# A graph layer with a mixture of experts: eleven dense sets of four tiles in place of thirteen

## The reference, cut to what matters

```python
h = layernorm(x) @ W
x = x + segment_sum(h[dst] * edge_weight[:, None], src) + bias
xn = layernorm(layernorm(x)) * gamma + beta
logits = xn @ Wr + br                       # 8 experts
w = softmax(top_2(logits))                  # spread over 8 columns, zero elsewhere
for e in range(8):
    y += (gelu(xn @ W1[e] + b1[e]) @ W2[e] + b2[e]) * w[:, e, None]   # 256 -> 512 -> 256
x = x + y
```

## Time and profile before

| | |
|---|---|
| median of 3 runs | 3774.95 us (3774.81 to 3778.23) |
| the profiled execution | 3771.83 us, of which 3770.1 us span |
| mean granted TensorE clock | 0.933 |
| busy in the span | TensorE 86%, VectorE 66%, GpSimd 64%, ScalarE 36% |

### The profile page before, as it was taken

The page is one execution under the profiler, slowest core; times in us unless marked ns, Lnnn a source line. Parts: engine busy times, 40 slices in busy tenths (PEclk is TensorE's granted clock), DMA queues, the critical chain, the costliest instruction groups (busy, mean ns, idle before and its releaser), DMA issues. The chain is left out here.

```text
span 3770.1 us, 77968 instructions
## 1 busy us (share of the span) xinstructions
PE 3237.5 (86%) x21468; PEld 2119.4 (56%) x21468; DVE 2486.9 (66%) x6355; ACT 1339.0 (36%) x2814; POOL 2402.3 (64%) x2251
## 2 busy tenths in 40 slices
PE   6679777644799999999999999999999999999997
PEld 3445444422455555555555555555555555567886
DVE  9699655534666676667666676666676667655664
ACT  1353766630122222223222222222222222255664
POOL 1151388877766766666667667676667676674555
PEclk8899888876899999999999999999999999999999
DMA  4342010103333333333334333333333333454554
GB/s 151 98 131 71 27 26 25 26 14 89 110 104 105 107 103 107 104 107 100 110 94 117 95 111 105 102 104 107 101 105 109 102 108 103 122 157 99 90 88 67
DMA packets 258290, 358.36 MB, mean 95 GB/s; under 512 B 86661, under 2 KB 199370, under 8 KB 257994
## 3 DMA queue, kind: packets, MB, share of 16 engines
q0 software_dynamic: 108032, 247.79, 25.2%
q1 hardware_dynamic: 106968, 64.44, 6.4%
q10 hardware_dynamic: 42996, 42.43, 3.5%
HBM read 290.79 MB, written 63.57 MB: 94 GB/s over the span
## 5 line engine op out<-in xcount | busy, mean ns | idle before, releaser
L804 POOL DMA_INDIRECT area<-h_table,listed x1664 | 1672.3, 1005 | 748.8 <-issue 482.4
L1901 PE MATMUL twin<-area 128*128 x2800 | 1024.1, 410 | 174.5 <-issue 148.8
L1903 PE MATMUL twin<-area 128*128 x2800 | 811.1, 290 | 0.0
L977 ACT ACTIVATE area<-twin,b_t 128x512 f32<-128x512 f32 x208 | 142.9, 687 | 1340.9 <-PE twin L1954 793.8
L1901 PEld LDWEIGHTS twin<-area 128*128 x2800 | 289.9, 104 | 575.6 <-issue 336.3
L1434 DVE TENSOR_TENSOR area<-area,listed 128x1024 f16 x700 | 453.2, 689 | 114.5 <-DVE area L1426 98.0
L772 POOL DMA_INDIRECT edge_list<-area,didx x256 | 326.6, 1276 | 76.2 <-issue 76.2
L1423 DVE TENSOR_SCALAR rel<-listed,tile_no 128x8 f16 x350 | 83.4, 238 | 418.2 <-issue 365.4
L1903 PEld LDWEIGHTS twin<-area 128*128 x2800 | 289.6, 103 | 60.3 <-issue 0.4
L1971 PE MATMUL bank<-w2h,area 128*128 128x256 f16 x1664 | 304.7, 273 | 0.0
L831 POOL DMA_INDIRECT out_dram<-area,put_row x108 | 185.2, 1715 | 164.2 <-DMA out_dram<-area,put_row 73.0
(11 more groups left out here) (381 smaller groups left out, 6190.7 us busy)
## 6 DMA issues: line engine op xcount, KB each, us to landing
area<-h_table,listed POOLq DMA_INDIRECT x1664
area<-in_x_dram SPq DMA_DIRECT2D x194, 128.0 KB, 2.2
area<-zs SPq DMA_DIRECT2D x54, 260.0 KB, 2.8
h_table<-area SPq DMA_DIRECT2D x97, 128.0 KB, 1.7
xt<-in_x_dram ACTq DMA_DIRECT2D x97, 128.0 KB
area<-in_L_ffn_W_dram ACTq DMA_DIRECT2D x16, 512.0 KB, 4.0
out_dram<-area ACTq DMA_DIRECT2D x12, 512.0 KB
out_dram<-area ACTq DMA_DIRECT2D x46, 128.0 KB, 2.8
```

The costliest lines, as they stand in the source:

```text
L804: pool.indirect_dma_start(out=stage[:, (k % RU) * UNIT + 2 * D * c:(k % RU) * UNIT + 2 * D * (c + 1)], out_offset=None, in_=h_table[:, :], ...
L1901: nc.tensor.matmul(psA[:, :], target[:, ds(at, P, 2)], stage[:, ds(rows, 2 * D)], start=False, stop=False)
L1903: last = nc.tensor.matmul(psA[:, 0:D], target[:, ds(at + TGT // 2, P, 2)], stage[:, ds(rows, D)], start=False, stop=False)
```

## The change

The sets begin every nine tiles in place of every eight: at 0, 9, ... 81 and at 94, 11 sets. So 44 tiles are dense and 54 are routed. An expert's step is looked up in a table, `expert_at`; a step that is not in it has no expert: steps 12, 21, ... 84, and 93 to 97. The loop has 107 steps in place of 109, and 88 experts in place of 104. Routed tiles lie in runs of five (the last of nine), and one iota for each run writes their row numbers. The wait of the transposes for the weights of a set counts the sets begun. The routing tables share one scratch tile in place of two, with the same operations in another order.

```diff
-    begins = list(range(0, NT - 2 * SB + 1, 2 * SB)) + [NT - SB]
+    begins = list(range(0, NT - 3 * SB, 2 * SB + 1)) + [NT - SB]
...
+    expert_at = {b + SB + e: c * NE + e for c, b in enumerate(begins) for e in range(NE)}
+    STEPS = max(expert_at) + 2
+    expert_at[STEPS - 1] = NEX
...
-            nc.gpsimd.iota(out_row[:, :, :], pattern=[[2 * SB * P, NQ], [P, SB]], base=SB * P - PAD,
-                           channel_multiplier=1).then_inc(s_rows_i, 1)
+            for t, n in spans:
+                nc.gpsimd.iota(out_row[:, place_of[t]:place_of[t] + n], pattern=[[P, n]], base=t * P - PAD,
+                               channel_multiplier=1).then_inc(s_rows_i, 1)
...
-            for t in range(NEX + SB):
-                i = t - SB
+            for t in range(STEPS - 1):
+                i = expert_at.get(t, -1)
...
-                route(nc.vector.tensor_tensor(behind_n[:, :, :], behind[:, :, :],
+                route(nc.vector.tensor_reduce(block_e[:, :], behind[:, :, :], AX.X, ALU.add))
+                route(nc.vector.tensor_tensor(behind[:, :, :], behind[:, :, :],
                                               blocks_f[:, :].unsqueeze(1).to_broadcast([P, NBL, NE]), ALU.mult))
-                route(nc.vector.tensor_reduce(block_e[:, :], behind[:, :, :], AX.X, ALU.add))
-                route(nc.vector.tensor_reduce(block_s[:, :], behind_n[:, :, :], AX.X, ALU.add))
+                route(nc.vector.tensor_reduce(block_s[:, :], behind[:, :, :], AX.X, ALU.add))
...
             def transposes(t):
-                c = (t - SB) // (2 * SB)
-                if c >= 0:
-                    pe.wait_ge(s_wT, min(c + 1, NSET))
+                reached(pe, s_wT, len([b for b in begins if b + SB <= t]))
...
-            for t in range(NEX + SB + 1):
-                i = t - SB
+            for t in range(STEPS):
+                i = expert_at.get(t, -1)
                 if t < NT:
                     chunks(t)
```

More of the change, by code:

```diff
@@ L119, in gnn_moe_layer_kernel @@
     OUT_ROW, SECOND, FIRST_MORE, FIRST_E = D, D + 1, D + 2, D + 3
-    NQ = -(-NR // SB)
-    assert all(routed[j] == 2 * SB * (j // SB) + SB + j % SB for j in range(NR)) and begins[0] == 0
+    spans = [(t, len([r for r in routed if t <= r and all(k in place_of for k in range(t, r))]))
+             for t in routed if t - 1 not in place_of]
+    assert begins[0] == 0 and begins[-1] == NT - SB and all(b - a >= 2 * SB for a, b in zip(begins, begins[1:]))
+    assert sum(n for _, n in spans) == NR
     ctx = ExitStack()
@@ L189, in gnn_moe_layer_kernel @@
         slot_i = sb("slot_i", [P, NR, 2], i32)
-        out_row = sb("out_row", [P, NQ, SB], i32)
+        out_row = sb("out_row", [P, NR], i32)
         dummy_row = sb("dummy_row", [P, 2], i32)
@@ L204, in gnn_moe_layer_kernel @@
         behind = sb("behind", [P, NBL, NE], fp32)
-        behind_n = sb("behind_n", [P, NBL, NE], fp32)
         block_e = sb("block_e", [P, NBL], fp32)
@@ L210, in gnn_moe_layer_kernel @@
         fill_i = sb("fill_i", [P, NE], i32)
-        earlier_i = behind_n[:, :, :].rearrange("p n e -> p (n e)")[:, 0:2 * NBL].bitcast(i32).rearrange(
+        earlier_i = behind[:, :, :].rearrange("p n e -> p (n e)")[:, 0:2 * NBL].bitcast(i32).rearrange(
             "p (k n) -> p k n", k=2)
-        earlier_f = behind[:, :, :].rearrange("p n e -> p (n e)")[:, 0:NBL]
+        earlier_f = behind[:, :, :].rearrange("p n e -> p (n e)")[:, 2 * NBL:3 * NBL]
         is_first = sb("is_first", [P, 2], fp32)
@@ L1630, in routed_weights @@
                 route(nc.vector.tensor_tensor(tw_r[:, :, 1], ex_r[:, :], tw_r[:, :, 0], ALU.mult))
-                nc.vector.tensor_copy(meta[:, :, 0].bitcast(i32), out_row[:, :, :].rearrange("p q s -> p (q s)")[:, 0:NR])
+                nc.vector.tensor_copy(meta[:, :, 0].bitcast(i32), out_row[:, :])
                 nc.vector.tensor_copy(meta[:, :, 1], tw_r[:, :, 1])
@@ L1692, in _ @@
             dve.wait_ge(s_hmm, NT)
-            dve.wait_ge(s_rows_i, 2)
+            dve.wait_ge(s_rows_i, len(spans) + 1)
             route(nc.vector.memset(zero_b[:, :, :].rearrange("p a w -> p (a w)"), 0.0))
```

## The result

The changed kernel takes 3800.72 us (median) against 3775.34 for the kernel before on the same chip, a ratio of 1.0069 [1.0054, 1.0084]. It is slower, by 25 us; the forecast was 3816, 41 more than the median of before, so the result lies in the lower part of the range (3796 to 3836).

What follows compares the result with a forecast made beforehand. TensorE was taken to bound the tile loop, then GpSimd's scatter, nearly balanced with the expert tail, then the blocks. Terms -31 + 21 + 49 + 2 = +41 us gave 3813, or 3816 as median; range 3796 to 3836.

Steps and rivals of the forecast that it cites:

- tile loop: Loop up to the scatter's start: shorter steps, set starts and routed tiles, less late gathers; 31 us less, bounds 6 and 59.
- scatter: GpSimd after its last gather: sixteen more scatters at 1.33 us each, all on the path, 21 us more.
- to the first add (restart): First block: TensorE, idle some 45 us ahead of it, may start at the lower clock; 0 to 5 us, 2 taken.
- blocks: Block loop at the end: 62 blocks in place of 54 at 6.1 us each, 49 us more, bounds 46 and 53.
- A missing expert gives 2.7 us, not 10.5: Tile steps without an expert: latency from tile sum to logits stays uncovered, so nine single steps give 24 us.
- The rival by which TensorE's work comes off in full: Steps 12 to 94 without an expert: each gives 10.5 us, total 50 us less, 3725; chance 0.05.
- Steps 93 to 96: Last tiles: 93 and 94 give 5 us; 95 and 96 nothing, as GpSimd gathers at its own pace after tile 95.
- Late gathers: Tile loop: shorter steps use up GpSimd's lead, so gathers may be late; 5 us more, bounds 0 and 30.
- Set starts and routed tiles: Tile loop: ten set starts beside tiles, not twelve, 4.4 us less; eight tiles turned dense to routed, 2.5 us less.
- A hidden growth: Rival at the scatter: its growth is hidden because ring waits shrink; total 20 us more, 3795; chance 0.04.
- 46 us: Lower bound for the eight added blocks, from TensorE's busy time alone, 5.7 us a block.
- The signs: Signs of being wrong: stretches without an expert under 7 us, gathers releasing line 1901 mid-loop, first block before 3410 us.

Runs made afterwards that it cites:

- cover: Changed kernel, with the second layer of a set's last expert run in the step without an expert, not the step after; 3773.13 us, 0.9994 of the kernel before.
- clumped: Changed kernel with its 11 sets begun every eight tiles, so steps with a tile and no expert all stand at the end; 3806.94 us, 1.0091 of the kernel before.
- blocks54: Changed kernel without its last eight blocks (54 run, not 62; their output rows missing); 3750.22 us, 0.9937 of the kernel before.

## Why the prediction was right, and where its terms were off

Term by term, from the stages of the two profiles:

| term | predicted | measured |
|---|---|---|
| tile loop | -31 | -34.3 |
| scatter | +21 | +19.0 |
| to the first add (restart) | +2 | +1.1 |
| blocks | +49 | +52.3 |
| ends and start | 0 | -5.8 and +3.5 |
| sum | +41 | +35.9 |

- *A missing expert gives 2.7 us, not 10.5.* Right. The nine bare stretches take 9.55 us on the mean where the same steps took 12.46, two of them set starts: 2.9 each, 26 us against 24. One of them (step 48) gave only 0.7 (12.77 to 12.06), since VectorE came 4.4 us late. cover shows the reason: with 5.2 us of work put into the idle time the stretch did not grow. The rival by which TensorE's work comes off in full is out.
- *Steps 93 to 96.* Right, and by the path that was named. GpSimd's last wait for buffer space ends in the sum of tile 95, before and after:
```profile
3238.36 0.94 POOL L804 DMA_INDIRECT area<-h_table,listed  x1 [6.75 <-SPq L686]
3206.99 0.94 POOL L809 DMA_INDIRECT area<-h_table,listed  x1 [3.06 <-SPq L690]
```
  From there to the first scatter it is 50.8 us before and 51.4 after. So the 5.4 us that the stretches of 95 and 96 became shorter (24.1 to 18.8) lie beside this path and bring nothing, as predicted; those of 93 and 94 lie on it and gave 5.7 (23.9 to 18.2) against 5.
- *Late gathers.* This is where the loop was mis-sized. 5 us were set aside; the sums up to that wait grew by 0.6, and the way from it to the scatter by 0.6. The last gather came 32.8 us earlier (about 30 predicted).
- *Set starts and routed tiles* were predicted at 4.4 and 2.5. Together with the bare steps they lie in stretches 5 to 92, which fell by 29.9 (1074.3 to 1044.4), 31 predicted.
- *Scatter.* Right: 108 in 140.3 us, 1.3 each, none of it covered. TensorE idled 45.1 us ahead of the first block, over 40 predicted. A hidden growth is out.
- *Restart.* 1.1 us, and 0.2 to 1.1 in the six profiles with 62 blocks, against 2. Over the first 8.8 us of the blocks the granted clock is 0.50, the lower of the two levels, after 45 us of idling, and the first four transposes take 1.09 us in place of 0.63. But before it was 0.61 over that time too, so there was less to lose.
- *Blocks.* The size was right, the reason not. The stage grew by 52.3 us here and by 50.0 on the mean of six profiles, against 49. The prediction took TensorE's 309 busy us of 336 for what sets the pitch. The chain of waits of the kernel before says otherwise; its shares by line, from the first add to the 107th:
```profile
by line: DMA out_dram<-area,put_row 57.2%; POOL out_dram L831 21.2%; issue 10.4%; POOLq L828 2.8%; PE twin L2041 1.5%; PE bank L2041 1.2%; PE twin L2058 1.2%; PE bank L2058 1.2%; DVE area L1737 1.2%; DVE area L1730 0.4%; PE twin L2025 0.4%;
```
  The adds and their landings hold 78% of it, TensorE's matmuls under 6%. So 46 us was no bound, and less work on TensorE need not make a block cheaper; no run here tried that. The sum did not suffer, because the price was read from the pitch.
- *What was missing* is the end: 10.9 us after the last add before, 5.1 after, in both profiles of the changed kernel. No term stood for it.
- The profiled sum of 35.9 is not the timed difference of 25 to 30, because single executions scatter: that of before lies 3.5 us under the median of its runs, that of after (3807.75) 7 above. 3.5 us of the sum lie ahead of the first tile's end, where nothing differs between the kernels that could explain it, and clumped shows 0.6. So of the 15 us by which 3816 was too high, 5 are the terms (41 against 35.9; the end of 5.8 is the largest error) and 10 are such scatter: 3.1 were added for the median of before, and the median of after lies 7 below its profile.
- *The signs.* Two that were named for being wrong came in all the same. The first block starts at 3405.53, earlier than 3410; but the prediction's own terms put it there (3416.94 - 31 + 21 = 3407), so the sign was set wrong and not the sum. And gathers released line 1906 (1901 before) four times in the middle of the loop, 3.8 us in all, where it was once, 0.3 us: there, but small.

## What to carry to other kernels

In a pipelined step, work taken off the busiest engine returns only what lies above the dependency chain that it covered. Measure that chain in a step that lacks the work already, as steps 1 and 2 here. When a step is emptied, look for other work whose order is free and that can stand in its idle time: a move of half an expert by one step was worth 31 us, more than the change itself cost. And an engine that looks late may be late because it works ahead for the next step; taking its lateness away in one step made the next pay more.

## What was not expected of the hardware

The time from the last add to the end of the span depends on the kernel, and not by chance: 10.9 to 11.0 us with 54 blocks (before, blocks54), 6.7 to 6.9 with 58, 5.0 to 5.1 with 62 in all six profiles of such kernels, 5.8 with 66. The trace has it on GpSimd: a drain behind the last add takes 6.7, 2.6, 0.9 and 1.5 us in them. Before and after (ns, start in us):
```profile
L124 POOLq DRAIN  x1: 6686/6686/6686, 3763.2 to 3763.2; - x1
L129 POOLq DRAIN  x1: 887/887/887, 3804.8 to 3804.8; - x1
```
Each time it stands behind the same two adds of 1.55 us. blocks54 differs from after in nothing else than the number of blocks, so that number, or something that goes with it, sets the drain; why, no run here shows. It made the change look 6 us cheaper than its work.
